# Value steps of an attention kernel: two products of each step change places, and four small loads and two subtractions move

## The chip, the cores and the metric

One core of one Trainium2 chip. The metric is the device time of one execution in microseconds (us). Engines: TensorE (PE; its weight loads are PEld), VectorE (DVE), ScalarE (ACT), GpSimd (POOL), SyncE (SP, which here only issues DMAs). Each engine runs its own list of instructions in order, and they wait for one another by semaphores.

## The reference

The input x has 64 groups of 32 tokens, 512 wide. All of it is float32.

```python
cond = einsum('bct,bcd->bdt', x, W[condition])          # tokens mixed within a group
q, k, v = cond @ Wq + bq, cond @ Wk + bk, cond @ Wv + bv  # inner width 4096: 32 heads of 128
q, k = rms_norm(q, gq), rms_norm(k, gk)                  # over all 4096
attn = softmax(q @ k.T / sqrt(128))                      # per head, within a group
x = x + (attn @ v) @ Wo + bo
# quantised weight with a low-rank part, then a mixture of low-rank experts
w_eff = dequantise(weight + lora_delta) + lora_delta     # 64 thresholds of a codebook
y = x @ w_eff.T
x = x + 2 * einsum('bshr,hor,bsh->bso', y @ A, Bm, 8 * softmax(y @ Wr + br))
```

## The kernel before

A float32 product is made of three matmuls: the operands are split in a high and a low part (`xs_hi`, `xs_lo` for the tokens, `wa` or `wv` for the weights), and hi*hi, hi*lo and lo*hi are added in PSUM. On top of that the q, k and v projections use a seven-product scheme for a 2 by 2 block product: seven products p1 to p7 give the four blocks 11, 12, 21 and 22, with additions on the other engines.

The projections take 96 steps. Steps s = 0 to 63 (`N_QK` = 64) make q and k, steps 64 to 95 (`N_ST` = 96) make v; u = s - 64 counts the latter. In a step

- TensorE does seven products, each six matmuls of 512 columns (twelve of 256 for u below 2 and above 29), in banks A (p1, p6, p7, p4), B (p5, p3) and C (p2). The order between the steps is written out by hand, and products of step s + 1 start before those of step s end.
- ACT copies bank A to SBUF after p1, p6 and p7 (`keep_a1`, `keep_a2`, `keep_a3`) and after p4 (block 21, line 1374).
- DVE adds these copies to the other banks: `block_11` (line 1762, after p2), `block_22` (line 1775, after p5, with a3) and `block_12` (line 1788, after p3, with a2). p3(s) adds onto bank B, so it waits for block_22(s).
- In the V steps SyncE stores each block to DRAM (`store_v`), and a block's buffer is written again only when its last store has landed.

V weights come in 8 groups (`QUADS`), one for each four steps. SyncE loads the raw group in two halves (`load_v_raw`), GpSimd makes four sums and differences (`add_v`), ACT rounds each of the seven operands (`split_v(j, q)`, line 1137), and GpSimd subtracts for the low part (`low_v(j, q)`, line 1558). In the first groups DVE does some of these (line 1634). A split waits until the product has used the group before. So the splits of one group fall at u = 4q - 4 (1, 2), 4q - 3 (6, 5, 7, 4) and 4q - 2 (3).

In the gaps DVE works through the codebook's thresholds, one level at a time: a `tensor_scalar` (line 1728) and a `tensor_tensor` (line 1729), both on 128 x 1024 values in SBUF. `levels_v` gives two or three levels a step for u from 5 to 27; three for even u and for u = 9, 13, 17, 21, 25. One stands before block_12, the others behind it.

TensorE's waits for weights: `weights_ahead` puts the wait for the next product's weights ahead of the last matmul of this one; its table says which product is next. For s below 2 and s = 64 to 66 the wait stands at the product itself.

`lora(1)` in step 66 needs `la` and `lbt`, which SyncE loads with four DMAs of 128 KB (lines 490 to 492), once the first half of the effective weight is done (`w_eff_done`).

Of the kernel before, what the change touches and what calls it, by code (L numbers as in the profile page):

```python
# [12 lines left out]
P = 128  # L13
# [97 lines left out]
def build(nc, x_nat, x_tr, cond_w, cond_idx, codebook, wqk, wv_in, wo_in, vecs, bo, w2, scale_log,  # L111
# [4 lines left out]
    with ExitStack() as ctx:  # L116
# [314 lines left out]
        def _(sp):  # L431
# [28 lines left out]
            def load_v_raw(g, half):  # L460
                if g == 0 and half == 0:

                    sp.wait_ge(w_lo[1], H)
                    sp.wait_ge(w_lo[4], H)
                    sp.wait_ge(s_added[3], H)
                    sp.wait_ge(s_added[4], H)
                elif g == 0:
                    for k in (6, 7, 3):
                        sp.wait_ge(w_lo[k], H)
                elif half == 0:  # L470

                    sp.wait_ge(v_lo[1], g)
                    sp.wait_ge(v_lo[2], g)
                    sp.wait_ge(sv_added[4], g)
                else:
                    sp.wait_ge(v_lo[4], g)
                    sp.wait_ge(v_lo[7], g)
                    sp.wait_ge(sv_added[4], g)
                sp.dma_start(wraw[:, half * 1024:(half + 1) * 1024], wv_in[V_ORDER[g]][:, half * 1024:(half + 1) * 1024])\
                  .then_inc(ld_vraw[half], 16)  # L480

            for s in range(1, N_QK):
                if s % 2 == 1 and (s + 3) // 2 < H:
                    load_raw((s + 3) // 2)
                if s == N_QK - 3:
                    load_v_raw(0, 0)
                if s == N_QK - 2:
                    load_v_raw(0, 1)
                    sp.wait_ge(w_eff_done, 1)
                    for rows in (slice(0, RANK), slice(RANK, P)):  # L490
                        sp.dma_start(la[rows], lora_a).then_inc(ld_lora[1], 16)
                        sp.dma_start(lbt[rows], lora_bt).then_inc(ld_lora[1], 16)
                if s % 2 == 0:
                    sp.wait_ge(kept, s // 2)
                    sp.dma_start(spill[s // 2 - 1], stage).then_inc(spilled, 16)
# [2 lines left out]
            sp.wait_ge(kept, H)  # L498
            sp.dma_start(spill[H - 1], stage).then_inc(spilled, 16)
            load_v_raw(1, 1)  # L500

            def store_v(s, c, done):
                u = s - N_QK
# [133 lines left out]
        def _(pe):  # L637
# [116 lines left out]

            def weights_ahead(s, j):

                if s <= N_QK:
                    s, j = {6: (s, 5), 5: (s + 1, 1), 1: (s - 1, 7), 7: (s + 1, 2), 2: (s - 1, 4), 4: (s, 3), 3: (s + 1, 6)}[j]
                else:
                    s, j = {6: (s - 1, 3), 3: (s + 1, 5), 5: (s + 1, 1), 1: (s - 1, 7), 7: (s + 1, 2), 2: (s - 1, 4), 4: (s + 1, 6)}[j]  # L760
                if s < N_ST and not first_weights(s):
                    weights_ready(s, j)

# [54 lines left out]
            def p3(s):  # L818
                weights(s, 3)
                if s < 2:  # L820
                    pe.wait_ge(x_act, x_act_at(2 * s + 1, 2))
                    pe.wait_ge(x_dve, x_dve_at(2 * s + 1, "l3"))
                pe.wait_ge(c22_done, s + 1)
                product(s, 3, bank_b(s), False)
# [100 lines left out]
            for s in range(N_QK, N_ST):  # L925
                if s > N_QK:
                    p6(s)
                    p3(s - 1)
                    p5(s)
                if s + 1 < N_ST:  # L930
                    p1(s + 1)
                if s == N_QK + 1:
                    norm_sums()
                if s == N_QK + 2:
                    pe.wait_ge(var_ready, 2)
                    lora(1)
                p7(s)
                if s + 1 < N_ST:
                    p2(s + 1)
                else:  # L940
                    pv(0)
                    pv(1)
                p4(s)
            p3(N_ST - 1)

            def project_out(b, outputs=range(KI)):
                c, p = b // NP, b % NP
# [136 lines left out]
        def _(act):  # L1084
# [253 lines left out]
            for s in range(N_QK, N_ST):  # L1338
                u = s - N_QK
                q, ahead = (u + 2) // 4, (u + 2) % 4 - 4  # L1340
                keep_a2(s)
                if ahead == -4 and 0 < q < QUADS:
                    split_v(3, q)
                if s == N_ST - 3:
                    exponent(0)
                if s == N_QK:
                    split_v(4, 0)
                    split_v(3, 0)
                if ahead == -1 and q + 1 < QUADS:
                    split_v(6, q + 1)  # L1350
                    split_v(5, q + 1)
                if s + 1 < N_ST:
                    keep_a1(s + 1)
                if s == N_ST - 2:
                    zero_pt(1)
                if ahead == -2 and 0 < q < QUADS - 1:
                    split_v(1, q + 1)
                keep_a3(s)
                if s == N_QK:
                    split_v(1, 1)  # L1360
                if ahead == -1 and q + 1 < QUADS:
                    split_v(7, q + 1)
                if ahead == -2 and 0 < q < QUADS - 1:
                    split_v(2, q + 1)
                if s == N_ST - 1:
                    for b in range(2):
                        out_hi(b, 0)
                        out_hi(b, 1)
                act.wait_ge(p_done[4], s + 1)
                if s == N_QK:  # L1370
                    act.wait_ge(acc_done, N_SQ - SQ_DIRECT)
                else:
                    act.wait_ge(v_stored[21], 16 * (s - N_QK))
                act.activation(v_out[21], bank_a(s)[:, :], ACT.Copy).then_inc(c21_done, 1)
                if s == N_QK:
                    split_v(2, 1)
                if ahead == -1 and q + 1 < QUADS:
                    split_v(4, q + 1)
                if s == N_ST - 4:
                    zero_pt(0)  # L1380
                if s == N_ST - 2:
                    split_o(0)
                if s == N_QK + 1:
                    act.wait_ge(var_ready, 1)
                    act.activation(qn[:, :], qv1n[:, :], ACT.Sqrt).then_inc(std_ready, 1)
                    act.wait_ge(var_ready, 2)
                    act.activation(kn, kv, ACT.Sqrt).then_inc(std_ready, 1)
# [216 lines left out]
        def _(dve):  # L1604
# [22 lines left out]
            def low_v(j, q):  # L1627

                dve.wait_ge(v_hi[j], q + 1)
                if q == 0 and j in (2, 5, 6):  # L1630
                    dve.wait_ge(p_done[{2: 5, 5: 7, 6: 4}[j]], N_QK)
                elif q == 0 and j == 7:
                    dve.wait_ge(scored, H)
                dve.tensor_tensor(wv_part(j, 1, q), v_raw[j], wv_part(j, 0, q).bitcast(F32), ALU.subtract).then_inc(v_lo[j], 1)
# [327 lines left out]
            for s in range(N_QK, N_ST):  # L1962
                u = s - N_QK
                block_22(s)
                if u == 0:
                    low_v(1, 1)
                if s + 1 < N_ST:
                    block_11(s + 1)
                if u == 0:
                    low_v(2, 1)  # L1970
                if u == 1:
                    variances()
                if u == 2:
                    keep_update(2)
                    keep_update(3)
                    norms()
                if u == 3:
                    key_norms()
                    dve.wait_ge(ld_quant[1], 16)
                    normalised(2)  # L1980
                if u == 29:
                    invert(0)
                if levels_v(s):
                    level(1, taken)
                    taken += 1
                if u == 30:
                    transpose_p(0)
                    transpose_p(1)
                if u == 31:
                    out_lo(0, 0)  # L1990
                    out_lo(0, 1)
                    transpose_p(2)
                    transpose_p(3)
                block_12(s)
                if u == 4:
                    normalised(3)
                    first_level(1)
                for _ in range(levels_v(s) - 1):
                    level(1, taken)
                    taken += 1  # L2000
                if u == 28:
                    shift(0)
                if u == 29:
                    straight_through(1)
                    effective(1)
                if u == 30:
                    shift(1)
# [166 lines left out]
```

## Time and profile before

| what | value |
|---|---|
| time, median of 3 runs | 1450.88 us (1450.84 to 1451.1) |
| the profiled execution | 1450.84 us, span 1449.0 us |
| granted TensorE clock | 1.000 |
| TensorE busy | 1444.1 us |
| DVE / ACT / GpSimd busy | 1070.7 / 726.7 / 746.3 us |

The span goes from the first to the last instruction; the device time is 1.8 us longer. The profile gives, for each instruction, its start from the start of the span, its length, the line that made it and, where its engine sat idle before it, what released it. Two instructions of one engine can overlap a little in the records.

### The profile page before, as it was taken

Reading aid. Unit: us, or ns where it says so; the run is one execution under the profiler, and the core shown is the slowest. Engines: PE = TensorE matmul, PEld = TensorE weight load, DVE = VectorE, ACT = ScalarE, POOL = GpSimd, SP = SyncE. Lnnn points to the kernel's source line nnn. Section 1 sums busy time; section 2 is a strip of 40 time slices with the busy share of each in tenths; the row PEclk is TensorE's granted clock in tenths of the full one; section 3 lists DMA queues with packets and bytes.
Section 4 is the critical chain, followed back from the end, with each engine's and each line's share of the span. In section 5 each row is a group of like instructions: output and inputs, shape, how many; then the busy total and the mean of one; then the engine's idle time right before and its main releaser. Section 6 shows DMA issues by size and latency. Waiting matters only on the chain.

```text
span 1449.0 us, 34717 instructions
## 1 busy us (share of the span) xinstructions
PE 1444.1 (100%) x14507; PEld 1201.0 (83%) x14507; DVE 1070.7 (74%) x1507; ACT 726.7 (50%) x1331; POOL 746.3 (52%) x530
## 2 busy tenths in 40 slices
PE   9999999999999999999999999999999999999999
PEld 8788888888888888888888888888888888888887
DVE  8787868687787877875468888988667667667663
ACT  7766676767766767676333333334342222222221
POOL 7668777777777877776345555514452111112100
PEclk9999999999999999999999999999999999999999
DMA  4211011110111011102443434447563334244230
GB/s 152 66 45 45 31 38 45 45 40 29 45 45 45 26 42 45 45 31 67 137 146 133 142 128 144 145 139 255 172 215 118 103 118 132 84 137 132 74 118 30
DMA packets 106989, 135.13 MB, mean 93 GB/s; under 512 B 6224, under 2 KB 89424, under 8 KB 106320
## 3 DMA queue, kind: packets, MB, share of 16 engines
q1 hardware_dynamic: 105968, 132.49, 27.8%
q8 instruction: 114, 1.87, 0.5%
q10 hardware_dynamic: 864, 0.42, 0.1%
q14 instruction: 43, 0.35, 0.1%
HBM read 86.75 MB, written 46.14 MB: 92 GB/s over the span
## 4 chain that ended last, share of the span: by engine, by line
PE 97%; DVE 1%; ACT 1%; issue 1%; DVEq 0%; POOL 0%; ACTq 0%; POOLq 0%
PE bank L713 41%; PE bank L960 25%; PE bank L732 21%; PE bank L918 4%; PE bank L844 3%; PE bank L988 1%; PE bank L1006 1%; PE bank L662 0%; DVE wa L1624 0%; PE bank L641 0%; DVE qreg L1708 0%; PE bank L974 0%; PE bank L1017 0%; ACT xs_hi L1160 0%; DVE sqst L1708 0%
## 5 line engine op out<-in xcount | busy, mean ns | idle before, releaser
L713 PE MATMUL bank<-xs_hi,wa 128*128 128x512 f32 x1792 | 563.3, 392 | 0.2
L1527 POOL TENSOR_TENSOR accr<-accr,sqst 128x512 f32<-128x512 f32 x248 | 353.3, 1435 | 148.0 <-ACT sqst L1197 107.6
L713 PEld LDWEIGHTS bank<-xs_hi,wa 128*128 128x128 f32 x1792 | 336.3, 188 | 74.0 <-DVE qk L1775 2.3
L713 PE MATMUL bank<-xs_lo,wa 128*128 128x512 f32 x896 | 348.7, 389 | 0.0
L960 PE MATMUL bank<-ot,wo_main 128*128 128x512 f32 x1344 | 316.6, 392 | 0.0
L960 PEld LDWEIGHTS bank<-ot,wo_main 128*128 128x128 f32 x1344 | 249.5, 188 | 52.6
L732 PE MATMUL bank<-wv,xs_hi 128*128 128x512 f32 (+1 forms) x1008 | 282.6, 366 | 0.1
L1624 DVE TENSOR_TENSOR wa<-wraw,wa 128x256 fp32r<-128x256 f32 (+1 forms) x160 | 156.8, 981 | 97.5 <-ACT wa L1106 95.7
L1322 ACT ACTIVATE ot<-bank,vec 128x256 fp32r<-128x256 f32 x256 | 100.4, 476 | 240.0 <-PE bank L960 146.8
L732 PEld LDWEIGHTS bank<-wv,xs_hi 128*128 128x128 f32 x1008 | 182.0, 189 | 33.0 <-issue 1.9
L1955 DVE SCALAR_TENSOR_TENSOR ot<-bank,vec,ot 128x256 fp32r<-128x256 f32 x256 | 106.2, 478 | 135.7 <-ACT ot L1322 135.4
L713 PEld LDWEIGHTS bank<-xs_lo,wa 128*128 128x128 f32 x896 | 168.3, 188 | 33.2
L732 PE MATMUL bank<-wv,xs_lo 128*128 128x512 f32 (+1 forms) x504 | 184.2, 365 | 0.0
L1570 POOL TENSOR_TENSOR wraw<-wraw,rinv 128x1024 f32<-128x1024 f32 x16 | 30.7, 1916 | 269.3 <-DVE rinv L1937 269.3
L1197 ACT ACTIVATE sqst<-qk 128x512 f32<-128x512 f32 x165 | 103.6, 628 | 61.4 <-DVE qk L1775 38.5
L1949 DVE STREAM_TRANSPOSE weights_b<-wraw 32x256 f32<-32x256 f32 x256 | 111.3, 435 | 3.5
L1775 DVE TENSOR_TENSOR qk<-bank,snap 128x512 f32<-128x512 f32 x96 | 66.1, 689 | 64.4 <-ACT snap L1187 28.6
L732 PEld LDWEIGHTS bank<-wv,xs_lo 128*128 128x128 f32 x504 | 95.0, 189 | 15.2
L1729 DVE TENSOR_TENSOR qreg<-qreg 128x1024 f32<-128x1024 f32 x63 | 103.9, 1650 | 2.2
L1729 DVE TENSOR_TENSOR accr<-accr,qreg 128x1024 f32<-128x1024 f32 x63 | 92.7, 1472 | 2.2
L1106 ACT ACTIVATE wa<-wraw 128x256 fp32r<-128x256 f32 (+1 forms) x160 | 79.1, 495 | 3.2 <-PE bank L713 3.2
L1176 ACT ACTIVATE snap<-bank,vec 128x512 f32<-128x512 f32 x64 | 44.2, 691 | 72.4 <-PE bank L713 72.4
(222 smaller groups left out, 1729.0 us busy)
## 6 DMA issues: line engine op xcount, KB each, us to landing
values_b<-v_spill SPq DMA_DIRECT2D x60, 512.0 KB, 4.7
wraw<-in_wqk SPq DMA_DIRECT2D x32, 512.0 KB, 3.5
v_spill<-qk SPq DMA_DIRECT2D x64, 256.0 KB, 2.3
v_spill<-sqst SPq DMA_DIRECT2D x64, 256.0 KB, 2.2
score_spill<-sqst SPq DMA_DIRECT2D x32, 256.0 KB, 2.0
wraw<-in_wv SPq DMA_DIRECT2D x16, 512.0 KB, 5.0
wraw<-score_spill SPq DMA_DIRECT2D x16, 512.0 KB, 4.1
spare<-in_wo SPq DMA_DIRECT2D x15, 512.0 KB, 5.3
```

The source lines that it names most:

```text
L713: ins = pe.matmul(dst[:, :], wa[:, col:col + P], xpart[:, j - 1, kt, n * CH:(n + 1) * CH], start=(first and k == 0), stop=(k == 5), skip_g ...
L732: ins = pe.matmul(out, xpart[:, j - 1, kt, t * P:(t + 1) * P], rhs, start=(first and k == 0), stop=(k == last), skip_group_check=True)
L960: ins = pe.matmul(bank[i][:, :], wo_slot(p)[:, wpart, col:col + P], ot[:, b % 2, opart, h, :], start=(p == 0 and k == 0), stop=(p == NP - ...
L1106: act.activation(wa[:, col:col + n], wraw[:, src:src + n], ACT.Copy).then_inc(w_hi[g], 1)
L1197: act.activation(dst, src, ACT.Square).then_inc(sq_ready, 1)
L1322: ins = act.activation(ot_part(ot[:, b % 2, 0, h, :], r), pv_part(b, r, h), ACT.Identity, bias=vec[:, 2 * (b % NP) + h, 2:3], scale=1.0)
L1527: pool.tensor_tensor(a, a, sq_slot(count), ALU.add).then_inc(acc_done, 1)
L1624: dve.tensor_tensor(wa[:, col + n:col + 2 * n], wraw[:, src:src + n], wa[:, col:col + n].bitcast(F32), ALU.subtract).then_inc(w_lo[g], 1)
L1729: link(dve.tensor_tensor(qf[half], qf[half], qm, ALU.add))
L1775: dve.tensor_tensor(dst, bank_b(s)[:, :], a3, ALU.add).then_inc(c22_done, 1)
L1949: ins = dve.transpose(pt[rows, b % 2, :, :, j * C:(j + 1) * C], src)
L1955: ins = dve.scalar_tensor_tensor(out=ot_part(ot[:, b % 2, 1, h, :], r), in0=pv_part(b, r, h), scalar=vec[:, 2 * (b % NP) + h, 2:3], in1=ot ...
```

## The change

On TensorE each V step has the order p6, p5, p1, p7, p2, p4, p3, as the q and k steps have, where p3 of a step came behind p6 of the next. `weights_ahead` has one table. ACT's split of operand 3 goes ahead of keep_a2. SyncE's lora loads go from step 62 to behind `load_v_raw(1, 1)`. On DVE low_v(1, 1) and low_v(2, 1) go behind block_12 of step 64.

```diff
--- before.py
+++ after.py
@@ -486,10 +486,6 @@
                     load_v_raw(0, 0)
                 if s == N_QK - 2:
                     load_v_raw(0, 1)
-                    sp.wait_ge(w_eff_done, 1)
-                    for rows in (slice(0, RANK), slice(RANK, P)):
-                        sp.dma_start(la[rows], lora_a).then_inc(ld_lora[1], 16)
-                        sp.dma_start(lbt[rows], lora_bt).then_inc(ld_lora[1], 16)
                 if s % 2 == 0:
                     sp.wait_ge(kept, s // 2)
                     sp.dma_start(spill[s // 2 - 1], stage).then_inc(spilled, 16)
@@ -498,6 +494,10 @@
             sp.wait_ge(kept, H)
             sp.dma_start(spill[H - 1], stage).then_inc(spilled, 16)
             load_v_raw(1, 1)
+            sp.wait_ge(w_eff_done, 1)
+            for rows in (slice(0, RANK), slice(RANK, P)):
+                sp.dma_start(la[rows], lora_a).then_inc(ld_lora[1], 16)
+                sp.dma_start(lbt[rows], lora_bt).then_inc(ld_lora[1], 16)
 
             def store_v(s, c, done):
                 u = s - N_QK
@@ -754,10 +754,7 @@
 
             def weights_ahead(s, j):
 
-                if s <= N_QK:
-                    s, j = {6: (s, 5), 5: (s + 1, 1), 1: (s - 1, 7), 7: (s + 1, 2), 2: (s - 1, 4), 4: (s, 3), 3: (s + 1, 6)}[j]
-                else:
-                    s, j = {6: (s - 1, 3), 3: (s + 1, 5), 5: (s + 1, 1), 1: (s - 1, 7), 7: (s + 1, 2), 2: (s - 1, 4), 4: (s + 1, 6)}[j]
+                s, j = {6: (s, 5), 5: (s + 1, 1), 1: (s - 1, 7), 7: (s + 1, 2), 2: (s - 1, 4), 4: (s, 3), 3: (s + 1, 6)}[j]
                 if s < N_ST and not first_weights(s):
                     weights_ready(s, j)
 
@@ -925,7 +922,6 @@
             for s in range(N_QK, N_ST):
                 if s > N_QK:
                     p6(s)
-                    p3(s - 1)
                     p5(s)
                 if s + 1 < N_ST:
                     p1(s + 1)
@@ -941,7 +937,7 @@
                     pv(0)
                     pv(1)
                 p4(s)
-            p3(N_ST - 1)
+                p3(s)
 
             def project_out(b, outputs=range(KI)):
                 c, p = b // NP, b % NP
@@ -1338,9 +1334,9 @@
             for s in range(N_QK, N_ST):
                 u = s - N_QK
                 q, ahead = (u + 2) // 4, (u + 2) % 4 - 4
-                keep_a2(s)
                 if ahead == -4 and 0 < q < QUADS:
                     split_v(3, q)
+                keep_a2(s)
                 if s == N_ST - 3:
                     exponent(0)
                 if s == N_QK:
@@ -1962,12 +1958,8 @@
             for s in range(N_QK, N_ST):
                 u = s - N_QK
                 block_22(s)
-                if u == 0:
-                    low_v(1, 1)
                 if s + 1 < N_ST:
                     block_11(s + 1)
-                if u == 0:
-                    low_v(2, 1)
                 if u == 1:
                     variances()
                 if u == 2:
@@ -1992,6 +1984,9 @@
                     transpose_p(2)
                     transpose_p(3)
                 block_12(s)
+                if u == 0:
+                    low_v(1, 1)
+                    low_v(2, 1)
                 if u == 4:
                     normalised(3)
                     first_level(1)
```

## Rows read from the trace of the kernel before

**Rows 1.** The page: span, busy time of each engine, the chain that ended last.
```profile
span 1449.0 us, 34717 instructions
PE 1444.1 (100%) x14507; PEld 1201.0 (83%) x14507; DVE 1070.7 (74%) x1507; ACT 726.7 (50%) x1331; POOL 746.3 (52%) x530
...
PE 97%; DVE 1%; ACT 1%; issue 1%; DVEq 0%; POOL 0%; ACTq 0%; POOLq 0%
```

**Rows 2.** Waits of PE (the longer of two entries): us in total, times, longest.
```profile
PE bank L641 <- POOL rqk L1461: 1.0, 1, 1.0
```

**Rows 3.** Windows, u = 12 to 15: busy us (instructions) by engine, clock, DMA share.
```profile
808.82:818.34 9.52, 9.52 (x43) 7.88 (x42) 8.17 (x8) 4.18 (x8) 7.21 (x5) 1.00 0.32 110
...
sum 38.08, PE 38.08 PEld 31.53 DVE 33.84 ACT 13.56 POOL 19.17; mean PE 9.52 PEld 7.88 DVE 8.46 ACT 3.39 POOL 4.79
```

**Rows 4.** Timeline of PEld behind p4(13): start, length (us), engine, line.
```profile
820.64 0.41 PEld L732 LDWEIGHTS bank<-wv,xs_hi 128*128 128x128 f32 x2
```

**Rows 5.** Timeline of DVE [idle before <-releaser]: u = 12, 13; 9; 25.
```profile
809.62 0.69 DVE L1775 TENSOR_TENSOR qk<-bank,snap 128x512 f32<-128x512 f32 x1 [0.94 <-ACT snap L1187]
...
810.82 0.81 DVE L1728 TENSOR_SCALAR qreg<-accr,thr,step 128x1024 f32<-128x1024 f32 x1
811.67 2.19 DVE L1729 TENSOR_TENSOR accr<-accr,qreg 128x1024 f32<-128x1024 f32 x1
814.32 0.69 DVE L1788 TENSOR_TENSOR sqst<-bank,snap 128x512 f32<-128x512 f32 x1 [0.45 <-PE bank L732]
814.92 1.01 DVE L1728 TENSOR_SCALAR qreg<-accr,thr,step 128x1024 f32<-128x1024 f32 x1
815.97 1.23 DVE L1729 TENSOR_TENSOR accr<-accr,qreg 128x1024 f32<-128x1024 f32 x1
817.23 1.67 DVE L1728 TENSOR_SCALAR qreg<-accr,thr,step 128x1024 f32<-128x1024 f32 x1
...
820.19 0.69 DVE L1775 TENSOR_TENSOR qk<-bank,snap 128x512 f32<-128x512 f32 x1
...
782.12 0.69 DVE L1775 TENSOR_TENSOR qk<-bank,snap 128x512 f32<-128x512 f32 x1
...
934.43 0.69 DVE L1775 TENSOR_TENSOR qk<-bank,snap 128x512 f32<-128x512 f32 x1
```

**Rows 6.** Timeline in a q and k step, p3 behind p4: block_22 and the load.
```profile
178.17 0.68 DVE L1775 TENSOR_TENSOR qk<-bank,snap 128x512 f32<-128x512 f32 x1
...
178.90 0.19 PEld L713 LDWEIGHTS bank<-xs_hi,wa 128*128 128x128 f32 x1 [0.21 <-DVE qk L1775]
```

**Rows 7.** Timeline of ACT: the split of operand 6, behind keep_a2(13).
```profile
813.39 0.62 ACT L1137 ACTIVATE wv<-qreg 128x512 fp32r<-128x512 f32 x1
```

**Rows 8.** Timeline of POOL: low_v of operands 6 and 5.
```profile
814.09 1.29 POOL L1558 TENSOR_TENSOR wv<-qreg,wv 128x512 fp32r<-128x512 f32 x1 [1.31 <-ACT wv L1137]
816.39 1.96 POOL L1558 TENSOR_TENSOR wv<-qreg,wv 128x512 fp32r<-128x512 f32 x1 [1.00 <-ACT wv L1137]
```

**Rows 9.** SyncE's DMA issues at steps 62 to 64; below, issues: KB, us to landing.
```profile
667.66 0.33 SPq L479 DMA_DIRECT2D wraw<-in_wv  x1
...
671.08 0.58 SPq L495 DMA_DIRECT2D score_spill<-sqst  x1
...
689.57 0.33 SPq L479 DMA_DIRECT2D wraw<-in_wv  x1
...
score_spill<-sqst SPq DMA_DIRECT2D x1, 256.0 KB, 3.2
...
v_spill<-qk SPq DMA_DIRECT2D x1, 256.0 KB, 4.1
```

**Rows 10.** Timeline of DVE: block_11(65).
```profile
694.43 0.69 DVE L1762 TENSOR_TENSOR qk<-bank,snap 128x512 f32<-128x512 f32 x1 [1.71 <-DMA v_spill<-qk]
```

**Rows 11.** Timeline of POOL: the third addition of the second group.
```profile
696.83 1.29 POOL L1507 TENSOR_TENSOR wraw<-wraw 128x512 f32<-128x512 f32 x1
```

**Rows 12.** Timeline of PEld: p1(66) begins.
```profile
697.18 0.31 PEld L732 LDWEIGHTS bank<-wv,xs_hi 128*128 128x128 f32 x2
```

## The prediction

> **What bounds the kernel now.** I read the page's busy line and its chain first. TensorE is busy 1444.1 of 1449.0 us and holds 97% of the chain that ended last, at full clock [rows 1, 3]. The reader should see that nothing can be won beyond about 5 us, and that whatever the change costs must show as TensorE standing still. The list of all TensorE's waits has two entries, the longer of 1.0 us at the very start [rows 2], so the stage that the diff touches (the V stage, steps s = 64 to 95; I write u = s - 64) has no stall of its own now. The table by windows of one period of four steps, u = 12 to 15, gives the step: 9.52 us, always TensorE-bound (seven products of 1.36 us). DVE is busy 8.17 us of it at u = 12 and 8.46 on the average of the four [rows 3]. So the question is not how much work moves, but whether DVE still delivers each block before TensorE asks for it, now that TensorE asks in another order.
>
> **What the change does.** (a) On TensorE, in each of 31 steps, p6(s) and p3(s-1) change places. p3(s-1) runs one product (1.36 us) earlier, p6(s) one later; the other five stay where they are. No instruction is added or removed. (b) ACT's split_v(3, q) goes ahead of keep_a2; (c) the table of waits for the next product's weights follows the order; (d) SyncE's four lora loads go from step 62 to behind load_v_raw(1, 1), ahead of the first block's store; (e) DVE's low_v(1, 1) and low_v(2, 1) go behind block_12 of step 64. (b) and (c) cost nothing: the weights are finished microseconds ahead (GpSimd has a group's operand 5 at 818.35 [rows 8], and p5(14), the first to use it, comes one step of 9.52 behind p5(13)'s end, which let the split go), and if that cover went, a wait would stand right at p3.
>
> **The step in detail, and the margin it has.** p3(s) waits for block_22(s) on DVE, line 1775. I take step u = 13. The first weight load of the product behind p4(13) starts at 820.64 [rows 4]. That product is p6(14) now and will be p3(13). DVE's block_22(13) runs from 820.19 to 820.88 [rows 5]. Left where it is, it would be 0.24 us late, plus the hand-over. For the hand-over there is a case in the first stage, where p3 follows p4 as in the new order: block_22 ends at 178.85 and the weight load starts at 178.90 [rows 6]: 0.05 us, so 0.29 late in all. Steps in which DVE does not run behind have room: block_22(12) starts at 809.62, released by ACT, and p3(12) would want its weights one step ahead of 820.64, at 811.12, 0.8 us after it ends.
>
> **What DVE does with the earlier p3.** Before block_12(12) DVE waits 0.45 us for p3(12) [rows 5]. That wait goes, since p3(12) ends 1.36 us earlier, and alone it would put block_22(13) in time by 0.16. But p6(13) ends 1.36 later, and with it keep_a2(13) and, behind it, split_v(6), from 813.39 to 814.75, done 815.37 [rows 7]. So GpSimd's low_v(6), now at 814.09 in a moment when DVE reads PSUM, comes at 815.45, when DVE is in a level. The rows show what that costs. A GpSimd subtraction alone takes 1.29. One that starts while a DVE level instruction runs ends 1.15 after that instruction (817.20 to 818.35). The next DVE level instruction then takes 1.67 where alone it takes 0.81 (817.23 against 810.82), or 2.19 where alone it takes 1.23 (811.67 against 815.97), about 0.9 more [rows 5, 8]. The blocks, which read PSUM, take 0.69 either way. The walk from rows:
> block_12(12) 813.89; level 814.50 to 815.31; 815.34 to 816.57, with low_v(6) waiting from 815.45 and running to 817.72; level 816.60 + 1.67 = 818.27, with low_v(5) waiting behind it (its data is there by 816.39) to 819.42; level 818.30 + 2.19 = 820.49; block_22(13) 820.53 to 821.22.
> Against 820.64 less 0.05 that is 0.63 late. In the order of before only one GpSimd operation was pushed between these levels (817.23), and 0.2 of another (814.92); now two are, 0.75 more than before, for 0.45 saved.
>
> The Trainium skill says of this port ("SBUF — State Buffer", "Who interferes with whom") that a DVE instruction with two SBUF inputs or in a 2-port mode and a GpSimd instruction that reads SBUF lock each other out for the whole instruction, whoever starts first. The rows agree but for its length: the level at 814.92 ends at 815.94, so it began about 0.26 before low_v(6)'s recorded end. By the rule to the letter each of the two pushes would cost 0.26 more, and the time would be that of rival 3.
>
> **How often.** It needs a step with three levels behind another with three, and a GpSimd group in it: u = 9, 13, 17, 21, 25. block_22 runs in all five behind DVE's own work in the same way, 782.12 the first and 934.43 the last (five) [rows 5]. Five times 0.6 is 3.0 us. In the steps behind them (10, 14, ...) DVE has three levels too, but TensorE has then just been held 0.6, and the p3 ahead of their levels is early as well: I take nothing. Bounds for one of the five: 0 (GpSimd's two fall where DVE reads PSUM) and 1.04 (the two of them without the 0.45 saved, 0.29 + 0.75); for all five 0 to 5.2. The term is nearest to the rows of 811.67 and 817.23, so 3.0.
>
> **The lora loads and the two low_v.** From the raw load at step 62 to the DMA behind the four lora loads SyncE takes 671.08 - 667.66 = 3.42 us [rows 9]. Behind load_v_raw(1, 1) (689.57) the same four put the store of block 11 of step 64, now at 690.17, at 692.99. DVE's block_11(65) waits for its landing already: it starts at 694.43 after 1.71 idle [rows 10]. The spill at 671.08 landed 3.2 after its issue behind the same loads [rows 9]; so block_11(65) starts at about 696.2. Behind it, new, come block_12(64) at 696.8 and only then low_v(1, 1) at 697.4. GpSimd's additions run there; the one at 696.83 is 1.29 long [rows 11] and, let go 0.26 before its end as at 814.09, holds it till 697.9, so it ends at 698.5. p1(66) wants these weights: its first load stands at 697.18 [rows 12]. It starts 1.4 late. Bounds: 0 (the store lands within 2.2 of its issue, and nothing pushes in: 697.1), and 2.8 (landing 4.1, as the store at 690.17 now [rows 9], and one push of 0.9 in low_v). I take 1.4, by the landing behind the same loads. Queued behind SyncE's loads are this store and those after it; behind low_v(2, 1) DVE has no level to do in these steps, and p2(66), which wants it, comes 4 us later, behind the norm sums and p7(65). At step 62 the loads leave a gap that hides nothing: no wait of TensorE is there.
> p7(s) has one product less between it and p6(s), whose a2 ACT keeps in 0.6: 2.7 us are left, 1.4 in the last step. Nothing.
>
> **Sum.** 3.0 + 1.4 = 4.4. The profiled run took 1450.84 us (span 1449.0 and 1.8 around it), the median is 1450.88: 1455.2 us. No change that is smaller than 0.2% (2.9 us) counts as one here.
>
> **Rivals.**
> 1. Only the start costs. GpSimd's operations fall between the blocks and the early p3 is hidden: 1450.84 + 1.4 = 1452.2. For it: the walk turns on 0.1 us (low_v(6) at 815.45 against a level at 815.34), and without a second push block_22(13) is in time. Against: had GpSimd come first, the level would wait instead of GpSimd, which is the same 0.9. Chance 0.24.
> 2. Nothing is felt, the other side of my forecast: the lora loads land with no delay, so low_v(1, 1) is ready before 697.1 and the steps hide theirs. It decides from a landing within 2.2 us of the issue. The time: 1450.8; TensorE has some 5 us of idle in the whole span [rows 1], and none of it lies at a p3 or p6 of these steps. Chance 0.09, of it 0.02 for a gain that can be told.
> 3. The port is held longer than I read it. If each push costs 0.26 more, which is what low_v(6)'s recorded end would give at 814.92, a step is late by 0.63 + 0.52 = 1.15 and five by 5.8: 1450.84 + 5.8 + 1.4 = 1458.0. For it: low_v(6) is recorded to 815.38. Against: the level at 814.92 is done at 815.93, 0.81 is its length, so it was let in at 815.12, before that end. Chance 0.07. This is what the Trainium skill's rule above comes to.
> The forecast: 0.60. Slower by over 0.2% is the forecast and rival 3: 0.67. Within it rivals 1 and most of 2: 0.31. Faster 0.02. The range leaves out rival 3 and most of rival 2: 1451.6 to 1457.2; the forecast's own range is 1453.8 to 1457.2.
>
> **What would show it.** TensorE's list of waits gets an entry of five for line 1775 of some 3 us, at the steps 9, 13, 17, 21, 25, each period of four steps 38.7 for 38.08 us, and one wait of p1(66) for line 1634 of about 1.4. block_11(65) starts near 696.2. DVE's wait before block_12(12) is gone, and two level instructions of 1.7 and 2.2 stand between block_12(12) and block_22(13). Wrong would make it: a block_22(13) that ends before 820.6, no idle weight load there, or a store that lands before 695.2.

## The result and the profile after

The changed kernel takes 1459.3 us (median of 4 runs, 1458.02 to 1461.37), the kernel before 1450.86: a ratio of 1.0059, 95% interval 1.0042 to 1.0078. It is slower, as forecast, but by 8.4 us instead of 4.4, and above the range. Its runs spread over 3.3 us, those of the kernel before over 0.6. The profiled execution is shorter than all four: 1457.52 us, span 1455.7 against 1449.0.

TensorE's list of waits, in us in total, times and longest:

```profile
PE bank L732 <- DVE wv L1630: 2.2, 1, 2.2
PE bank L732 <- DVE qk L1771: 1.3, 5, 0.3
PE bank L641 <- POOL rqk L1457: 1.0, 1, 1.0
```

The two new entries are the two that the prediction names: p1(66) waits once for a low_v on DVE (line 1634 before, 1630 here), and p3 waits five times for block_22 (1775 before, 1771 here). This list counts only the time in which no matmul is in flight. From first matmul to first matmul the costs are larger, as the timelines show. First TensorE at p1(66), to be set beside [rows 12]. Before the change p1(66) and, further on, p7(65) start so:

```profile
697.30 0.63 PE L732 MATMUL bank<-wv,xs_hi 128*128 128x512 f32 x2
...
700.84 0.50 PE L732 MATMUL bank<-wv,xs_hi 128*128 128x256 f32 x2
```

After it:

```profile
697.21 0.28 PE L732 MATMUL bank<-wv,xs_lo 128*128 128x256 f32 x1
699.66 1.22 PE L732 MATMUL bank<-wv,xs_hi 128*128 128x512 f32 x2 [2.17 <-DVE wv L1630]
700.67 0.63 PE L732 MATMUL bank<-wv,xs_lo 128*128 128x512 f32 x1
701.10 1.05 PE L732 MATMUL bank<-wv,xs_hi 128*128 128x512 f32 x2
701.95 0.63 PE L732 MATMUL bank<-wv,xs_lo 128*128 128x512 f32 x1
...
704.78 0.51 PE L732 MATMUL bank<-wv,xs_hi 128*128 128x256 f32 x2
```

The matmul due at 697.33 (697.30, and the 0.03 by which this execution is late before the wait) starts at 699.66: 2.33 us. The ones behind it are 0.43 us apart, where they are 0.23 apart elsewhere. p7(65), the product behind p1(66) and the norm sums, starts at 704.78 and did at 700.84: 3.94 later. So 1.6 us are lost behind the wait; of them 0.1 are lost at full clock too, as later runs show, and 1.5 are the clock's. The table by windows shows why (busy us by engine, clock, DMA share, GB/s):

```profile
697.00:699.70 2.70, 0.53 (x6) 0.33 (x4) 2.00 (x4) 0.77 (x2) 2.70 (x3) 0.99 0.16 53
699.70:703.20 3.50, 3.50 (x64) 2.46 (x67) 1.59 (x1) 0.58 (x1) 2.72 (x2) 0.52 0.54 189
703.20:706.00 2.80, 2.80 (x110) 1.96 (x99) 0.00 (x0) 0.02 (x1) 0.00 (x0) 1.00 0.03 6
```

The granted clock falls to half, 1.2 GHz, as TensorE begins to work again after 2.3 us of standing still, and is back at 2.4 GHz 3.4 us later. Standing still has a price of its own.

Now the step u = 13, DVE's timeline from block_22(12) to block_22(13), GpSimd's, and the weight load of p3(13), which answer to [rows 4, 5, 8]:

```profile
814.08 0.69 DVE L1771 TENSOR_TENSOR qk<-bank,snap 128x512 f32<-128x512 f32 x1 [1.35 <-ACT snap L1183]
...
816.12 2.20 DVE L1725 TENSOR_TENSOR accr<-accr,qreg 128x1024 f32<-128x1024 f32 x1
818.36 0.69 DVE L1784 TENSOR_TENSOR sqst<-bank,snap 128x512 f32<-128x512 f32 x1
818.96 0.81 DVE L1724 TENSOR_SCALAR qreg<-accr,thr,step 128x1024 f32<-128x1024 f32 x1
819.80 1.23 DVE L1725 TENSOR_TENSOR accr<-accr,qreg 128x1024 f32<-128x1024 f32 x1
821.07 1.66 DVE L1724 TENSOR_SCALAR qreg<-accr,thr,step 128x1024 f32<-128x1024 f32 x1
822.76 2.19 DVE L1725 TENSOR_TENSOR accr<-accr,qreg 128x1024 f32<-128x1024 f32 x1
824.99 0.69 DVE L1771 TENSOR_TENSOR qk<-bank,snap 128x512 f32<-128x512 f32 x1
```

```profile
819.92 3.96 POOL L1554 TENSOR_TENSOR wv<-qreg,wv 128x512 fp32r<-128x512 f32 x2 [2.68 <-ACT wv L1133]
```

```profile
824.87 0.19 PEld L732 LDWEIGHTS bank<-wv,xs_lo 128*128 128x128 f32 x1
825.74 0.30 PEld L732 LDWEIGHTS bank<-wv,xs_hi 128*128 128x128 f32 x2 [0.68 <-DVE qk L1771]
```

DVE's wait before block_12(12) is gone, and the walk holds instruction for instruction: from block_12 to block_22 it takes 6.63 us (818.36 to 824.99), 6.64 in the prediction. The load of p3(13) follows the end of block_22 by 0.06. What the five waits cost together is read from a matmul ahead of the first and one behind the last, before and after the change (the first of each pair is before):

```profile
768.50 0.62 PE L732 MATMUL bank<-wv,xs_hi 128*128 128x512 f32 x2
772.42 0.61 PE L732 MATMUL bank<-wv,xs_hi 128*128 128x512 f32 x2
...
945.98 0.62 PE L732 MATMUL bank<-wv,xs_hi 128*128 128x512 f32 x2
952.71 0.61 PE L732 MATMUL bank<-wv,xs_hi 128*128 128x512 f32 x2
```

TensorE is 3.92 us late ahead of them and 6.73 behind them: 2.8 us, 0.54 to 0.59 at each.

The account of this execution: 2.3 of waiting, 1.6 behind it and 2.8 at the five p3 are the 6.7 us of span.

### The profile page after: what moved, and what is told of

The parts are those of the page before. It is cut to its first block, busy times and chain, and to the rows that moved or that the text cites. A ratio compares the mean times of both kernels' runs of the same rounds, so it can differ in the third digit from the quotient of the medians.

```text
span 1455.7 us, 34717 instructions
## 1 busy us (share of the span) xinstructions
PE 1447.5 (99%) x14507; PEld 1201.8 (83%) x14507; DVE 1082.1 (74%) x1507; ACT 726.5 (50%) x1331; POOL 750.7 (52%) x530
## 4 chain that ended last, share of the span: by engine, by line
PE 47%; DVE 4%; issue 0%; ACT 0%; DVEq 0%
PE bank L956 24%; PE bank L732 16%; PE bank L915 4%; DVE accr L1725 2%; DVE qreg L1724 1%; PE bank L984 1%; PE bank L1002 1%; DVE qk L1771 0%; PE bank L1013 0%; PE bank L970 0%; DVE sqst L1784 0%; DVE qk L1758 0%; ACT snap L1183 0%; PE bank L1034 0%; PE bank L851 0%
## 5 line engine op out<-in xcount | busy, mean ns | idle before, releaser
L1725 DVE TENSOR_TENSOR accr<-accr,qreg 128x1024 f32<-128x1024 f32 x63 | 101.5, 1611 | 2.2
```

The source lines that it names most:

```text
L1725: link(dve.tensor_tensor(qf[half], qf[half], qm, ALU.add))
```

## The experiments

There were twelve runs, in three groups of four, each group on one chip together with the kernel before: e1 to e4 (kernel before 1451.60), e5 to e8 (1450.72), and the other four (1450.63). "More" is the difference of the medians to the kernel before of the same group, in us. The expectations count from 1450.9, so across groups "more" is the figure to compare.

| kernel | median (runs) | more | ratio, 95% interval |
|---|---|---|---|
| e1, lora loads back | 1454.51 (11) | 2.9 | 1.0022, 1.0013 to 1.0030 |
| e2, low_v back | 1454.49 (11) | 2.9 | 1.0023, 1.0014 to 1.0031 |
| e3, order only | 1455.26 (11) | 3.7 | 1.0023, 1.0014 to 1.0032 |
| e4, wait filled | 1457.80 (5) | 6.2 | 1.0043, 1.0030 to 1.0056 |
| e5, start only | 1454.96 (6) | 4.2 | 1.0032, 1.0020 to 1.0043 |
| e6, levels moved | 1461.31 (5) | 10.6 | 1.0073, 1.0061 to 1.0085 |
| e7, short low_v | 1450.60 (11) | -0.1 | 0.9998, 0.9990 to 1.0007 |
| e8, store first | 1454.15 (11) | 3.4 | 1.0024, 1.0016 to 1.0033 |
| changed kernel again | 1458.51 (5) | 7.9 | 1.0056, 1.0043 to 1.0068 |
| e9, start only, filled | 1453.84 (11) | 3.2 | 1.0023, 1.0014 to 1.0031 |
| e10, split late | 1453.51 (11) | 2.9 | 1.0018, 1.0009 to 1.0026 |
| e11, filled long | 1458.75 (5) | 8.1 | 1.0055, 1.0041 to 1.0069 |

**e1: the loads go back.** In the changed kernel:

```diff
                 if s == N_QK - 2:
                     load_v_raw(0, 1)
+                    sp.wait_ge(w_eff_done, 1)
+                    for rows in (slice(0, RANK), slice(RANK, P)):
+                        sp.dma_start(la[rows], lora_a).then_inc(ld_lora[1], 16)
+                        sp.dma_start(lbt[rows], lora_bt).then_inc(ld_lora[1], 16)
...
             load_v_raw(1, 1)
-            sp.wait_ge(w_eff_done, 1)
-            for rows in (slice(0, RANK), slice(RANK, P)):
-                sp.dma_start(la[rows], lora_a).then_inc(ld_lora[1], 16)
-                sp.dma_start(lbt[rows], lora_bt).then_inc(ld_lora[1], 16)
```

> The changed kernel, with the four lora loads back at step 62. Theory: the store of block 11(64) is issued 2.8 us earlier and lands as before, block_11(65) starts near 694.4, low_v(1, 1) is done before 697.1, so p1(66) waits 0 to 0.3 us and TensorE stays at 2.4 GHz. Left are the five waits of p3, 2.6 us: 1453.5 (1453.0 to 1454.2), with a spread of runs as small as that of the kernel before. Rival (the low_v behind block_12 are the cause of the long wait, whatever the loads do): p1(66) waits over 1 us here, and the time is 1455 or more.

The wait of p1(66) is gone from TensorE's list, and the clock is 1.000 in every run. The five waits of p3 are left. So the theory on the start holds. The median is 0.3 above the band. But on this chip the kernel before is 0.7 slower than the expectation took it; to that it is 2.9 more, where 2.6 was expected. The runs spread over 2.1 us, which the expectation did not have; e10 takes that up.

**e2: the two low_v go back.**

```diff
                 block_22(s)
+                if u == 0:
+                    low_v(1, 1)
                 if s + 1 < N_ST:
                     block_11(s + 1)
+                if u == 0:
+                    low_v(2, 1)
...
                 block_12(s)
-                if u == 0:
-                    low_v(1, 1)
-                    low_v(2, 1)
```

> The changed kernel, with low_v(1, 1) ahead of block_11(65) and low_v(2, 1) behind it, as before; the lora loads stay behind load_v_raw(1, 1). Theory: low_v(1, 1) no longer stands behind block_11(65), which still waits for its store till 697.7. p1(66) finds its weights ready and waits 0; block_12(64) and low_v(2, 1) come at 698 to 700, early enough for p2(66) and p5(66). 1453.5, as with the loads undone. Rival (the late landing delays something else too, as ACT's keep_a1(66) or the store buffers): TensorE waits over 0.5 us elsewhere between 697 and 716, and the time is above 1454.5.

The store still lands late here, block_11(65) starts at 696.99, and low_v(2, 1) behind it, pushed back, ends at 699.14. But TensorE has no wait between 697 and 716, and the time is that of e1. The long wait needs both moves: a late landing, and a low_v that stands behind it.

**e3: the order alone** (both of the edits above).

> Both the lora loads and the two low_v as before; only the order of the products, its table of weights and ACT's split_v(3) are changed. Theory: five waits of p3 of about 0.5 us and nothing else: 2.6 us, 1453.5, the same as with either one undone. Rival (the order itself makes the big part, through the clock): above 1455, and a window with a granted clock below 1.

The rival's clock is out: 1.000 in all eleven runs. The median is 1.1 us more than expected (3.7 for 2.6), and the runs lie in two clusters, four from 1453.6 to 1454.4 and seven from 1455.2 to 1455.8.

**e4 and e11: the wait is filled with matmuls.** In the changed kernel, 10 and 20 of them:

```diff
             def p1(s):
+                if s == N_QK + 2:
+                    pe.wait_ge(c21_done, s - 1)
+                    for _ in range(10):
+                        pe.matmul(bank_a(s)[:, :], xs_hi[:, 0, 0, 0:P], xs_hi[:, 0, 0, 0:CH], start=True, stop=True)
                 weights(s, 1)
```

> The changed kernel, with ten matmuls of 128x512 on data at hand ahead of p1(66), in its own bank, which p1 then overwrites. They take 2.3 us and fill the wait; p1(66) starts when it did or up to 0.2 later. Theory (the half clock from 699.8 to 703.2 comes of the 2.2 us in which TensorE stood still): the clock stays at 2.4 GHz, the time falls by 1.6 us from the profiled 1457.5, to 1455.9 (1455.5 to 1456.5), and the spread of the runs falls below 0.6 us. Rival (the clock falls for another reason, or the spread is DMA's): no gain, 1457.5 to 1461.

> The changed kernel with twenty matmuls of 128x512 ahead of p1(66), 4.5 us. They are longer than the wait, so p1(66) starts 4.5 us late whatever DVE does. Theory: nothing is left to wait for, clock 1.000 in all runs, and the time is the order-only kernel's (1453.6 to 1455.8) plus 4.5: 1458.1 to 1460.3; the half clock in the changed kernel costs as much as two more microseconds of standing still. Rival (the start hides part of such a delay, the norm sums or p7(65) would wait anyway): below 1457.5.

In both, every run is at clock 1.000. e4's time is above its band. Part of that is its chip (0.7). In its profile, one of its two longest runs, the store took 0.4 us more to land than in the changed kernel, low_v(1, 1) was pushed, and p1(66) waits 1.3 us more behind the filling. As a measure of what the clock costs it is inconclusive (6.2 more, against 8.4 and 7.9 for the changed kernel on two other occasions); that the clock stays up is plain. e11's median came as expected: 4.5 us of useless matmuls cost as much as the wait does (8.1 against 7.9).

**e5 and e9: the start alone, open and filled.** e5 is the kernel before with the lora loads and the two low_v moved, and e9 adds the ten matmuls.

> The kernel before, with only the lora loads and the two low_v moved, as in the change; the products keep their old order. Theory: no wait of p3. p3(64) runs one product later, but the landing at 697.7 sets the pace: p1(66) waits 2.2 us, the clock falls for some 3 us, so 1450.9 + 3.9 = 1454.8, up to 1457, with the wide spread of the changed kernel. Rival (each part hurts only with the other): 1450.9 to 1452.

> The kernel before with the lora loads and the two low_v moved (its runs: 1453.2 to 1453.7 at clock 1, 1456.2 to 1458.7 at 0.998 and 0.996), and ten matmuls of 128x512 ahead of p1(66) to fill its wait. Theory (what makes those runs longer is TensorE at half clock for some us after it stood still for 2.3): all runs at clock 1.000, 1453.2 to 1454.8, none above 1455.5. Rival (the fall of the clock has another cause): half of the runs at 0.996 to 0.998 as there, up to 1459.

This pair is the clean test of the clock, though on two chips. e5's six runs, with the granted clock of each: 1453.15, 1453.41 and 1453.71 at 1.000; 1456.21 at 0.998; 1457.83 and 1458.70 at 0.996. e9's eleven are all at 1.000 and between 1453.14 and 1455.31. So the wait costs 2.7 us (e5's middle run at full clock, less 1450.72), and the fall of the clock 2.8 to 5.3 us more, in half of e5's executions; two of these are above the 1457 that was expected at most. In e5's profile no clock fell, and the matmuls behind the wait are 0.23 apart:

```profile
699.16 0.73 PE L732 MATMUL bank<-wv,xs_hi 128*128 128x512 f32 x2 [2.34 <-DVE wv L1634]
699.73 0.39 PE L732 MATMUL bank<-wv,xs_lo 128*128 128x512 f32 x1
```

So a wait of 2.34 us by TensorE's list came without the fall, and one of 2.17, in the changed kernel, with it: the length of the wait does not decide. Over all runs, 11 of the 16 with the open wait of p1(66) (e5, and the changed kernel on both occasions) show a mean clock below 1, none of the 21 with the wait filled, and none of the 66 of e1, e2, e3, e7, e8 and e10, which have no such wait. Only e6, whose waits at p3 are long, has two more, at 0.999. The Trainium skill ("TensorE: Matmul & The Clock Gate", Part 1) has the half rate as the idle state and activity as what releases it. The runs agree: filled, no run falls.

**The changed kernel again.**

> The changed kernel once more, on the chip of the other three. Theory: 1458 to 1461 with a spread of over 2 us; the runs in which the granted clock is below 1 are the longer ones. Rival: the spread has nothing to do with the clock, and runs at clock 1 are as long as the others.

By clock: 1457.38 at 1.000; 1457.51 and 1458.51 at 0.999; 1459.07 at 0.998; 1461.52 at 0.996. The longer the lower. (The changed kernel's first runs are less orderly: 1458.02 at 1.000 against 1457.52 at 0.999.) The profiled one of these is at 1.000, and its span is still 1455.6, since one of its five waits of p3 is a long one:

```profile
PE bank L732 <- DVE qk L1771: 2.7, 5, 1.7
PE bank L732 <- DVE wv L1630: 2.4, 1, 2.4
```

Its p1(66) and p7(65), without a fall of the clock:

```profile
699.61 0.73 PE L732 MATMUL bank<-wv,xs_hi 128*128 128x512 f32 x2 [2.40 <-DVE wv L1630]
...
703.27 0.51 PE L732 MATMUL bank<-wv,xs_hi 128*128 128x256 f32 x2
```

This execution is 0.25 ahead of the kernel before until the wait. So p1(66) is 2.56 late and p7(65) 2.68: only 0.1 is lost behind the wait. The matmul that stands at 945.98 in the kernel before is at 952.54. With the 0.25 that is 6.81 late, so the five p3 cost 4.1 us here. The two make 6.8 us, and with them the changed kernel is above the forecast range of 1457.2 without any fall of the clock, here at 1457.38 and in the first runs at 1458.02.

**e8: the store ahead of the loads.** In the changed kernel the four lora loads stand behind the store of block 11(64) instead of ahead of it.

> The changed kernel, with the lora loads one place later on SyncE, behind the first store of block 11 (step 64). Theory (the store lands late because the loads are ahead of it, 2.2 us by its issue and 1.1 by its way): the store lands at 694.3, p1(66) waits at most 0.3 us, the clock stays, 1453.5. The store of block 22(64) is now behind the loads, but its buffer is wanted one step later. Rival (loads and stores share the DMA engines, so it is the same whichever is first): landing after 696, a wait of p1(66) over 1 us, 1455 or more.

The store is issued at 689.91 and lands 4.6 us later, half a us more than the 4.1 of the kernel before: the loads behind it are felt a little too. block_11(65) starts at 694.59, and p1(66) is not in TensorE's list. So it is the place in SyncE's queue that made the store late. The median is 3.4 more, where 2.6 was expected. In the changed kernel:

```profile
689.97 0.48 SPq L499 DMA_DIRECT2D qreg<-in_lora_a  x1
...
692.41 0.60 SPq L512 DMA_DIRECT2D v_spill<-qk  x1
```

```profile
697.70 0.69 DVE L1758 TENSOR_TENSOR qk<-bank,snap 128x512 f32<-128x512 f32 x1 [5.55 <-DMA v_spill<-qk]
```

It was issued 2.2 us later and took 5.2 to land instead of 4.1.

**e7: two short subtractions.** Order only, with GpSimd's low_v of operands 6 and 5 at 32 of 512 columns from group 2 on; the low parts of v's weights are so left incomplete.

```diff
-                pool.tensor_tensor(wv_part(j, 1, q), v_raw[j], wv_part(j, 0, q).bitcast(F32), ALU.subtract).then_inc(v_lo[j], 1)
+                n = 32 if q >= 2 and j in (5, 6) else 512
+                pool.tensor_tensor(wv_part(j, 1, q)[:, 0:n], v_raw[j][:, 0:n], wv_part(j, 0, q)[:, 0:n].bitcast(F32),
+                                   ALU.subtract).then_inc(v_lo[j], 1)
```

> Order only, with GpSimd's low_v of operands 6 and 5 of groups 2 to 7 cut to 32 of 512 columns; the rest of these low parts is left as it was, so v is not split fully. Theory (the two subtractions pushed between DVE's levels make block_22 late): each push costs DVE 0.1 to 0.3 us and not 0.9; block_22(13) ends before 820.6, no p3 waits: 1450.9. Rival (the margin is lost without GpSimd): five waits of 0.3 to 0.5 us stay, 1452.5 to 1453.5.

All waits of p3 are gone, and the time is that of the kernel before. DVE from block_12(12) to block_22(13):

```profile
813.85 0.69 DVE L1786 TENSOR_TENSOR sqst<-bank,snap 128x512 f32<-128x512 f32 x1
...
816.56 0.83 DVE L1726 TENSOR_SCALAR qreg<-accr,thr,step 128x1024 f32<-128x1024 f32 x1
817.43 1.22 DVE L1727 TENSOR_TENSOR accr<-accr,qreg 128x1024 f32<-128x1024 f32 x1
819.09 0.69 DVE L1773 TENSOR_TENSOR qk<-bank,snap 128x512 f32<-128x512 f32 x1 [0.44 <-ACT snap L1183]
```

The levels take 0.83 and 1.22 where they took 1.66 and 2.19, and block_22(13) now waits for ACT. This is shown: the two pushes are what p3 waits for, and without them the new order is free.

**e10: a race of a tenth of a microsecond.** Order only, with four tiny copies on ACT ahead of each split of operand 6.

```diff
+                if j == 6 and q >= 2:
+                    for k in range(4):
+                        at = 8 * (q - 2) + 2 * k
+                        act.activation(idx_i[:, at:at + 2].bitcast(F32), ones[:, 0:2], ACT.Copy)
                 act.activation(wv_part(j, 0, q), v_raw[j], ACT.Copy).then_inc(v_hi[j], 1)
```

> Order only, with four small copies on ACT ahead of the split of operand 6 in groups 2 to 7, so that GpSimd's low_v(6) comes some 0.5 us later and well inside DVE's level instead of within 0.1 us of its start. Theory (in the order-only kernel it is a race of 0.1 us whether GpSimd is let in before that instruction, which makes three pushes and a wait of 1.7 us instead of 0.4): always two pushes, every wait of p3 0.3 to 0.6 us, 1453.5 with a spread below 0.8 us. Rival (the runs spread for another reason): 1453.6 to 1455.8 as there.

Eleven runs between 1452.78 and 1453.67, a spread of 0.9 where below 0.8 was expected: the upper cluster of e3 is gone, by making an engine later. What the race decides is seen at u = 25. In e3, DVE and then GpSimd:

```profile
932.57 1.23 DVE L1725 TENSOR_TENSOR accr<-accr,qreg 128x1024 f32<-128x1024 f32 x1
933.83 1.66 DVE L1724 TENSOR_SCALAR qreg<-accr,thr,step 128x1024 f32<-128x1024 f32 x1
935.53 2.20 DVE L1725 TENSOR_TENSOR accr<-accr,qreg 128x1024 f32<-128x1024 f32 x1
...
932.68 3.96 POOL L1554 TENSOR_TENSOR wv<-qreg,wv 128x512 fp32r<-128x512 f32 x2 [2.67 <-ACT wv L1133]
```

and in e1, where this wait of p3 is 1.7 us:

```profile
931.88 2.30 DVE L1725 TENSOR_TENSOR accr<-accr,qreg 128x1024 f32<-128x1024 f32 x1
934.21 1.67 DVE L1724 TENSOR_SCALAR qreg<-accr,thr,step 128x1024 f32<-128x1024 f32 x1
935.91 2.33 DVE L1725 TENSOR_TENSOR accr<-accr,qreg 128x1024 f32<-128x1024 f32 x1
...
931.80 3.53 POOL L1554 TENSOR_TENSOR wv<-qreg,wv 128x512 fp32r<-128x512 f32 x2 [3.21 <-ACT wv L1133]
935.88 1.29 POOL L1554 TENSOR_TENSOR wv<-wraw,wv 128x512 fp32r<-128x512 f32 x1 [0.55 <-ACT wv L1133]
```

In e3 DVE's level starts 0.11 before GpSimd's low_v(6) and runs free. In e1 low_v(6) is 0.08 ahead, and that level is pushed. low_v(5) goes between it and the next, and then a third subtraction, of operand 7, is 0.03 ahead of the third level (935.88 against 935.91). Three pushes instead of two, 1.4 us on one wait. The profiles of e2 and of the changed kernel again show the same three pushes with the same 0.08.

That the upper cluster of e3 is the third push is inferred. Executions also differ by up to 0.8 us ahead of the V steps, where nothing was changed: block_22(64) starts at 691.43 in the kernel before, at 692.24 in e3 and at 690.85 in e2. So e2's profile has the long wait and e3's has not, and both are 1454.35.

**e6: the levels are shared out in another way.** Order only, and in `levels_v`:

```diff
-    return 3 if u % 2 == 0 or (u % 4 == 1 and u > 5) else 2
+    return 3 if u % 4 == 2 or (u % 4 == 1 and u > 5) or (u % 4 == 3 and u < 27) else 2
```

> Order only (as the run with both undone), with the levels shared out in another way: two in steps u = 8, 12, 16, 20 and 24 and three in u = 7, 11, 15, 19 and 23; the sum is 63 as before. Theory: DVE comes to block_22 of u = 9, 13, ... without the late run of the step ahead, so no p3 waits: 1450.9 (1450.5 to 1451.5). Rival (block_22 is late by what comes with p3's own place, not by the levels ahead of it): the five waits stay, 1453.5.

Both were wrong. The waits moved to u = 8, 12, 16, 20 and 24 and are of 1.3 to 2.6 us in TensorE's list. The two-level step now lies behind a three-level step (u = 7, 11, ...), in which GpSimd makes the four additions of a group. DVE in step 11:

```profile
802.50 1.71 DVE L1724 TENSOR_SCALAR qreg<-accr,thr,step 128x1024 f32<-128x1024 f32 x1
804.25 2.20 DVE L1725 TENSOR_TENSOR accr<-accr,qreg 128x1024 f32<-128x1024 f32 x1
...
808.18 2.20 DVE L1725 TENSOR_TENSOR accr<-accr,qreg 128x1024 f32<-128x1024 f32 x1
810.42 1.67 DVE L1724 TENSOR_SCALAR qreg<-accr,thr,step 128x1024 f32<-128x1024 f32 x1
...
813.38 0.69 DVE L1771 TENSOR_TENSOR qk<-bank,snap 128x512 f32<-128x512 f32 x1
```

Four instructions are pushed in one step. I read this so: it is not three levels behind three that makes a step late, but how many of GpSimd's operations meet its levels, and the kernel before is protected by having its two-level step there. No run tests this by itself.

## Why the prediction was wrong

The direction was right, and so were the two places at which TensorE waits. The time was 1459.3 against 1455.2 and outside the range. What failed is the size of the start, 1.4 where it was 2.4 to 2.7, and the sentence that "whatever the change costs must show as TensorE standing still": it put what the clock does behind a wait at nothing. A third error is the race at u = 25, which the prediction said to make no difference. By its steps:

- **p3 and block_22, five steps.** Right in place, number and mechanism (e7). The term was 3.0; it measured 2.8 in the profile, and 2.9 with the race ruled out (e10). The failed part is in rival 1: "had GpSimd come first, the level would wait instead of GpSimd, which is the same 0.9". When GpSimd comes first there is room for a third push, and one wait is 1.4 us longer: 4.1 for the term in the second profile of the changed kernel. e3's upper cluster, seven of eleven runs, goes away with the race, and its median is 3.7 with it. That those seven had the third push is inferred.
- **The start, 1.4.** This is the term that was mis-sized. p1(66) waits 2.33 in one profile of the changed kernel and 2.56 in the other; with the 0.1 behind it the start costs 2.4 to 2.7 (e5 at full clock: 2.7). SyncE's issue was 0.6 earlier than worked out (692.41 against 692.99), but the landing took 5.2, where 3.2 was taken, from the spill that stood behind the same loads in step 62. Here a spill of 256 KB more, issued at 688.50, was ahead as well; no run separates its part. The upper bound for the landing, 4.1, was wrong too: it came from a store without the loads ahead of it. low_v(1, 1) was not pushed in the profiled run, so p1(66) could go 2 us after block_11(65) began, where 2.4 were taken. That the term stayed below its upper bound of 2.8 is luck: the late landing was in part made up by the early issue and the missing push.
- **The clock, absent from the sum.** No term, bound or rival had what comes after a wait. It is 1.5 us in the profile, and in e5 2.8 to 5.3 in half of the runs. The rows of before could not show it, since TensorE's longest wait there is 1.0 us [rows 2].
- **The sum.** By medians, the order alone is 3.7 (e3) and the start at full clock 2.7 (e5): 6.4. The changed kernel is at 8.4 and 7.9, so 1.5 to 2 are left, which fits the clock. 6.4 alone is already at the upper end of the range (1457.2, 6.3 more than before).
- **Costed at nothing, and nothing:** the table of the next weights, ACT's split of operand 3, the loads leaving step 62, p7 with one product less ahead. None shows in TensorE's list in any of the twelve.
- **Rival 3**, the longer hold of the port, was wrong: the pushed instructions take 1.66 and 2.19, as before. Its time, 1458.0, was near the measured one for a reason that it did not name. Rival 1 is out by the five waits at p3, rival 2 by these and by the landing of 5.2.

What stays open: how the 3 to 5 us of the lowest clocks come about. Only one profile caught a fall, with 3.4 us at half clock. As an estimate from the mean clocks, 0.996 over 1457 us is 10 to 13 us at half clock and 0.998 is 4 to 7; whether these are one stretch or several, and where, no trace shows.

## What to carry to other kernels

When an engine that is always busy is made to wait, price the wait and then the clock behind it: here 2.3 us of waiting cost up to twice as much again, and filling the wait with useless matmuls was no worse than leaving it. When an operation is moved in a queue, bound its landing by a transfer that has all the same bytes ahead of it: here the landing with the four loads ahead (3.2) and the one with the spill and the raw load ahead (4.1) were both too low for the store that had all of these ahead of it (5.2). Where two engines push each other and the margin is some tenths, walk the instructions one by one, for both outcomes of the race, and count the pushes. Making one engine surely late can be better than making it early.

## What the runs showed of the hardware

- The granted clock fell to half for 3.4 us after TensorE, busy until then, stood still for 2.2 us (changed kernel, profiled). In e5, whose profile has a wait of 2.3 us in the same place, it stayed up in half of the executions, and with matmuls in the wait in all 21.
- GpSimd and DVE let each other in by turns, one operation each. 0.1 us decides whose turn is first: DVE's instruction of 1.23 takes 2.30 when GpSimd's subtraction starts 0.08 ahead of it, and 1.23 when that starts 0.11 behind.
- A store of 256 KB that lands 4.1 us after its issue lands 5.2 after it with four loads of 128 KB ahead, on top of the 2.2 us that SyncE takes to issue them, and 4.6 with them behind it.
